# Routed slots of a mixture of experts as pairs and single tiles, the singles in plain float32

## The reference, cut to what matters

```
gate = xt @ Wr + br                      # 1600 tokens, 7 experts
_, ids = top_k(gate + gate_bias, 2)
probs = softmax over the two selected logits
u  = einsum('nh,ehi->eni', xt, Wup) + bup
g  = silu(einsum('eni,eij->enj', u, Wgate) + bgate) * u
eo = einsum('enj,ejh->enh', g, Wdown) + bdown
out = einsum('ne,enh->nh', probs, eo)
out += shared expert of the same form (Wsu, Wsg, Wsd)
x = x + tanh(g_ffn[1]) * out
```

## Time and profile before

| | |
|---|---|
| median of 3 runs | 2024.52 us (2023.42 to 2028.41) |
| profiled execution | 2027.26 us, span 2025.5 us |
| TensorE busy | 1837.5 us, 91% |
| VectorE, ScalarE, GpSimd busy | 1398.9, 974.6, 680.3 us |
| HBM read, written | 156.99 MB, 33.36 MB |

### The profile page before, as it was taken

The page is one execution under the profiler, slowest core; times in us unless marked ns, Lnnn a source line. Parts: engine busy times, 40 slices in busy tenths (PEclk is TensorE's granted clock), DMA queues, the critical chain, the costliest instruction groups (busy, mean ns, idle before and its releaser), DMA issues. The chain is left out here.

```text
span 2025.5 us, 31266 instructions
## 1 busy us (share of the span) xinstructions
PE 1837.5 (91%) x11244; PEld 1445.7 (71%) x11258; DVE 1398.9 (69%) x2821; ACT 974.6 (48%) x2042; POOL 680.3 (34%) x628
## 2 busy tenths in 40 slices
PE   4899999999999899998987997999968899999996
PEld 4677887777877687777763544666538789999996
DVE  5776677777678677888767884677836437666664
ACT  3444444543544344443444654655433236666663
POOL 4332122332623212332101131232322564566553
PEclk9999999999999999999997998999979999999999
DMA  5022201220311321222125111000041457777783
GB/s 203 17 85 82 79 28 62 85 89 1 118 39 36 128 81 37 73 93 97 37 60 212 47 38 42 1 2 1 1 162 38 138 98 231 227 246 239 231 243 74
DMA packets 52397, 192.38 MB, mean 95 GB/s; under 512 B 7678, under 2 KB 11902, under 8 KB 41494
## 3 DMA queue, kind: packets, MB, share of 16 engines
q1 hardware_dynamic: 40550, 167.01, 23.5%
q0 software_dynamic: 11408, 23.37, 6.3%
q10 hardware_dynamic: 288, 0.00, 0.0%
HBM read 156.99 MB, written 33.36 MB: 94 GB/s over the span
## 5 line engine op out<-in xcount | busy, mean ns | idle before, releaser
L363 POOL TENSOR_TENSOR la_q_roped<-la_q_roped 128x400 f32<-128x400 f32 x128 | 139.5, 1111 | 682.5 <-DVE la_q_roped L819 682.5
L722 ACT ACTIVATE la_probs<-banks,la_minus_max 100x361 f32<-100x361 f32 x256 | 144.7, 565 | 195.1 <-DVE la_minus_max L909 195.1
L819 DVE TENSOR_TENSOR la_q_roped<-banks,la_rope_q 128x400 f32<-128x400 f32 x384 | 197.0, 565 | 26.7 <-PE banks L490 16.2
L2072 DVE TENSOR_TENSOR ex_weights_low<-ex_raw_weights,ex_weights_high 128x2048 fp32r<-128x2048 f32 x60 | 137.6, 2293 | 53.4 <-ACT ex_weights_high L1967 50.4
L527 PEld LDWEIGHTS banks<-identity,la_probs 100*121 100x121 f32 x768 | 113.0, 184 | 71.1 <-DVE la_probs L916 45.7
L916 DVE TENSOR_SCALAR la_probs<-la_probs,la_rsum 100x361 f32<-100x361 f32 x256 | 152.2, 595 | 9.1
L538 PE MATMUL banks<-la_probs_t,la_kv_rows 121*128 121x200 f32 x768 | 151.4, 333 | 0.0
L2339 POOL TENSOR_TENSOR ex_g_low<-ex_g,ex_g_high 128x256 fp32r<-128x256 f32 (+1 forms) x104 | 86.7, 950 | 179.1 <-ACT ex_g_high L2011 178.6
L909 DVE TENSOR_REDUCE la_minus_max<-banks 100x1 f32<-100x361 f32 x256 | 134.9, 527 | 16.1 <-PE banks L518 9.4
L527 PE MATMUL banks<-identity,la_probs 100*121 100x100 f32 x768 | 126.1, 273 | 21.8 <-DVE la_probs L916 18.2
L1967 ACT CAST ex_weights_high<-ex_raw_weights 128x2048 fp32r<-128x2048 f32 x60 | 114.2, 1903 | 41.8 <-PE banks L2420 35.1
(11 more groups left out here) (335 smaller groups left out, 5279.3 us busy)
## 6 DMA issues: line engine op xcount, KB each, us to landing
ex_raw_weights<-w_exp SPq DMA_DIRECT2D x60, 1024.0 KB
la_weights<-w_pack SPq DMA_DIRECT2D x15, 1856.0 KB, 7.9
la_kv_turned<-w_ffn SPq DMA_DIRECT2D x30, 384.0 KB
la_rope_k<-w_ffn SPq DMA_DIRECT2D x30, 384.0 KB
qf_sign_weights<-ffn_signs SPq DMA_DIRECT2D x3, 2048.0 KB, 10.2
ffn_signs<-la_ffn_signs SPq DMA_DIRECT2D x30, 192.0 KB, 2.1
residual<-x SPq DMA_DIRECT2D x2, 2048.0 KB, 14.4
out<-ex_block_out POOLq DMA_DIRECT2D x13, 256.0 KB, 5.0
```

The costliest lines, as they stand in the source:

```text
L363: pool.tensor_tensor(roped[:, h, 0, c, :], roped[:, h, 0, c, :], roped[:, h, 1, 1 - c, :], ALU.add).then_inc(b_add, 1)
L722: act.activation(prob[:, s % 4, 0:L], ps[0:S, s % 2, 0:L], ACT.Exp, bias=nmax[:, s % 4:s % 4 + 1], accum_out=sums[:, s % 4:s % 4 + 1]).the ...
L819: dve.tensor_tensor(roped[:, h, v, c, :].rearrange("p (b s) -> p b s", b=GB), ps[:, B_BANKS[k % 2], 0:NT].rearrange("p (b s) -> p b s", b=GB),
L2072: dve.tensor_tensor(wl[:, m, :], raw[:, m, :], wh[:, m, :].bitcast(F32), ALU.subtract).then_inc(w_low[m], 1)
```

## The change

The routed slots are 12 pairs (256 rows, as before) and 7 single tiles of 128, so 31 tiles where there were 38; still 19 blocks, in the order pair, single, pair, single, ..., then five pairs. An expert with an odd number of tiles has its last one in a single. Singles, and the shared block 6, use float32 operands and the unsplit weights: one matmul in place of three passes, no low parts. Their weights have a buffer of their own (`raw_s`) in the space of the residual, once that is stored, and each of their loads waits for the single before (its up, gate or down), in the same SyncE queue. `place` and `own` have more steps. SyncE's stores of normed rows come ahead of the first weight loads, which are issued after tiles 2, 6 and 10, and TensorE does not wait for all small loads at the start. In latent attention x is loaded as 4 + 4 + 8 tiles with norms in three parts, and the sign chunks stand at other places in VectorE's order.

```diff
-                sp.dma_start(core.x_all[:, 0:HB, :], x_in[:, 0:HB, :]).then_inc(x_loaded[0], 16)
+                sp.dma_start(core.x_all[:, 0:GB, :], x_in[:, 0:GB, :]).then_inc(x_loaded[0], 16)
                 sp.dma_start(wts[0][:, 0:W_R], w_pack[0, :, 0:W_R]).then_inc(w_first, 16)
+                sp.dma_start(core.x_all[:, GB:HB, :], x_in[:, GB:HB, :]).then_inc(x_loaded[1], 16)
                 sp.dma_start(trigk_all[:], rope_k).then_inc(tab_k, 16)
                 sp.dma_start(kv_all[:], ctx_in[0]).then_inc(kv_loaded, 16)
                 sp.dma_start(trig[:], rope_q).then_inc(tab_q, 16)
                 sp.dma_start(wts[0][:, W_R:W_ALL], w_pack[0, :, W_R:W_ALL]).then_inc(w_in[0], 16)
-                sp.dma_start(core.x_all[:, HB:B, :], x_in[:, HB:B, :]).then_inc(x_loaded[1], 16)
+                sp.dma_start(core.x_all[:, HB:B, :], x_in[:, HB:B, :]).then_inc(x_loaded[2], 16)
...
                 act.wait_ge(const_ready, 2)
+                std(0)
                 act.wait_ge(w_first, 16)
-                for w, high_part, _low in parts0:
+                for k, (w, high_part, _low) in enumerate(parts0):
                     act.copy(high_part, w).then_inc(w_high, 1)
-                std(0)
-                act.wait_ge(x_rstd, 6)
-                norm(0)
-                norm(1)
-                for t in range(GB):
-                    x_split(t)
-                    norm(t + 2)
+                    if k == 0:
+                        act.wait_ge(x_rstd, 6)
+                        norm(0)
+                        norm(1)
+                        for t in range(GB):
+                            x_split(t)
+                            if t + 2 < GB:
+                                norm(t + 2)
+                        std(1)
+                act.wait_ge(x_rstd, 12)
+                norm(GB)
+                norm(GB + 1)
...
                     rope(n, 0, 2)
+                    chunk(n, 0)
                     low(n, 2)
-                    chunk(n, 0)
                     rope(n, 1, 0)
                     rope(n, 1, 1)
+                    rope(n, 1, 2)
                     chunk(n, 1)
-                    rope(n, 1, 2)
...
                     rope(n, 2, 1)
-                    chunk(n, 2)
                     if n == 0:
-                        variances(1)
+                        variances(2)
                     if starts_half(n):
                         kv_split(n, 4)
                         kv_split(n, 5)
                     rope(n, 2, 2)
+                    chunk(n, 2)
...
-RB = E + (2 * N_TOK - E) // BN
-RT = 2 * RB
+RT = E + (2 * N_TOK - E) // BT
+NP = (RT - E) // 2
+NS = RT - 2 * NP
+RB = NP + NS
...
+def routed_order():
+
+    order = []
+    for k in range(max(NP, NS)):
+        order += [("pair", k)] * (k < NP) + [("single", k)] * (k < NS)
+    return order
+
...
+        old_x = core.x_all[:].rearrange("p b d -> p (b d)")
+        raw_s = old_x[:, 0:MATS * KC * D].rearrange("p (m w) -> p m w", m=MATS)
+        xs, us, gs = (old_x[:, at:at + KC * BT].rearrange("p (k n) -> p k n", k=KC)
+                      for at in range(MATS * KC * D, MATS * KC * D + 3 * KC * BT, KC * BT))
...
-                for m in range(MATS):
-                    load(E, m)
+                    sp.dma_start(bd[32 * k:32 * k + EA, :], b_down).then_inc(bd_in, 16)
+                for t in range(B):
+                    sp.wait_ge(normed[t % 2], t // 2 + 1)
+                    sp.dma_start(rows[t * S:(t + 1) * S, :], xn[:, t % XR, :]).then_inc(rows_out[t % XR], 16)
+                    if t in LOAD_AT:
+                        load(E, LOAD_AT.index(t))
+                    if t == 5:
+                        rows_of(0)
+                    if t == 8:
+                        rows_of(1)
...
+                sp.wait_ge(out_init, 64)
+                for m in range(MATS):
+                    sp.dma_start(raw_s[:, m, :], w_exp[E, m]).then_inc(s_in[m], 16)
                 sp.wait_ge(owners, 2)
-                for v in range(1, RB + 1):
-                    e = sp.value_load(owner_i[0:1, v - 1:v], min_val=0, max_val=E - 1)
+                for j in range(SH, BLOCKS):
+                    k = place_of(j)
+                    e = sp.value_load(owner_i[0:1, k:k + 1], min_val=0, max_val=E - 1)
                     for m in range(MATS):
-                        sp.wait_ge(w_low[m], v)
-                        sp.dma_start(raw[:, m, :], w_exp[bass.ds(e, 1), m].rearrange("e p d -> p (e d)")).then_inc(w_in[m], 16)
-                    if v == 1:
+                        if is_pair(j):
+                            sp.wait_ge(w_low[m], version_of(j))
+                            dst, arrived = raw[:, m, :], w_in[m]
+                        else:
+                            i = single_before(j)
+                            if m == UP:
+                                sp.wait_ge(u_psum, (i + 1) * KC)
+                            elif m == GATE:
+                                sp.wait_ge(g_psum, (i + 1) * KC)
+                            else:
+                                sp.wait_ge(d_psum, first_tile(i + 1))
+                            dst, arrived = raw_s[:, m, :], s_in[m]
+                        sp.dma_start(dst, w_exp[bass.ds(e, 1), m].rearrange("e p d -> p (e d)")).then_inc(arrived, 16)
...
                 def block_high(j):
                     act.wait_ge(t_psum, j + 1)
-                    act.copy(xbh[:, j % 2, :, 0:width(j)], turnb(width(j))).then_inc(xb_high, 1)
+                    if not is_pair(j) and singles_before(j) == 0:
+                        act.wait_ge(out_init, 64)
+                    dst = xbh[:, pairs_before(j) % 2, :, :] if is_pair(j) else xs
+                    act.copy(dst, turnb(width(j))).then_inc(xb_high, 1)
...
+                    step(dve.tensor_scalar(tiles[:], upto[:, :, B - 1], BT / 2 - 0.75, 1.0 / BT, ALU.add, ALU.mult))
+                    step(dve.tensor_scalar(tiles[:], tiles[:], ROUND, None, ALU.add))
+                    step(dve.tensor_scalar(tiles[:], tiles[:], ROUND, None, ALU.subtract))
+                    step(dve.tensor_scalar(pairs[:], tiles[:], 0.5, -0.25, ALU.mult, ALU.add))
+                    step(dve.tensor_scalar(pairs[:], pairs[:], ROUND, None, ALU.add))
+                    step(dve.tensor_scalar(pairs[:], pairs[:], ROUND, None, ALU.subtract))
+                    step(dve.scalar_tensor_tensor(out=odd[:], in0=pairs[:], scalar=-2.0, in1=tiles[:],
+                                                  op0=ALU.mult, op1=ALU.add))
+                    for end, n in ((pair_end, pairs), (odd_end, odd)):
+                        step(dve.tensor_tensor_scan(end[:], restart[:, 0, 1:1 + E], n[:], 0.0, ALU.mult, ALU.add))
+                    step(dve.tensor_tensor(pair_at[:], pair_end[:], pairs[:], ALU.subtract))
+                    step(dve.tensor_scalar(pair_at[:], pair_at[:], float(BN), None, ALU.mult))
+                    step(dve.tensor_tensor(odd_at[:], odd_end[:], odd[:], ALU.subtract))
+                    step(dve.tensor_scalar(odd_at[:], odd_at[:], float(BT), float(NP * BN), ALU.mult, ALU.add))
+                    step(dve.scalar_tensor_tensor(out=odd_at[:], in0=pairs[:], scalar=-float(BN), in1=odd_at[:],
+                                                  op0=ALU.mult, op1=ALU.add))
+                    step(dve.tensor_scalar(pair_rows[:], pairs[:], float(BN), -0.5, ALU.mult, ALU.add))
+                    step(dve.tensor_scalar(shift[:], odd_end[:, E - 1:E], float(BT), None, ALU.mult))
...
+                    step(dve.tensor_tensor(hit[:], earlier[:], each(pair_rows), ALU.is_le))
+                    step(dve.tensor_tensor(biased[:], earlier[:], each(pair_at), ALU.add))
+                    step(dve.tensor_scalar(logit[:], biased[:], NP * BN - 0.5, None, ALU.is_ge))
+                    step(dve.scalar_tensor_tensor(out=biased[:], in0=logit[:], scalar=shift[0:S, 0:1], in1=biased[:],
+                                                  op0=ALU.mult, op1=ALU.add))
+                    step(dve.tensor_tensor(earlier[:], earlier[:], each(odd_at), ALU.add))
+                    step(dve.tensor_tensor(biased[:], biased[:], earlier[:], ALU.subtract))
+                    step(dve.tensor_tensor(biased[:], biased[:], hit[:], ALU.mult))
+                    step(dve.tensor_tensor(earlier[:], earlier[:], biased[:], ALU.add))
...
+                    at, last = seq[:, E + NP:E + RB], odd_end[:, E - 1:E]
+                    step(dve.tensor_copy(index[:, 0:NP], seq[:, E:E + NP]))
+                    step(dve.tensor_scalar(index[:, NP:RB], at, last, None, ALU.subtract))
+                    step(dve.tensor_scalar(index[:, NP:RB], index[:, NP:RB], 0.5, -0.25, ALU.mult, ALU.add))
+                    step(dve.tensor_scalar(index[:, NP:RB], index[:, NP:RB], ROUND, None, ALU.add))
+                    step(dve.tensor_scalar(index[:, NP:RB], index[:, NP:RB], ROUND - NP, None, ALU.subtract))
```

(61 more changed lines are left out.)

209 lines of the change are left out of this document (121 added, 88 removed).

## The result

The changed kernel takes 1978.55 us (median of 4 runs, 1973.56 to 1981.05) where the kernel before takes 2024.83 (4 runs). The ratio is 0.9767, 95% interval 0.9749 to 0.9785: 43.5 to 50.8 us faster. The forecast was 1960, the range 1944 to 1986. The sign and the main mechanism hold, the time is inside the range, and the gain of 46 us is about 0.7 of the 65 that the sum promised.

What follows compares the result with a forecast made beforehand. The prediction took TensorE alone to bound the routed blocks, but not the stage's start. Terms -47 - 6 - 12 - 9 + 8.5 = -65.5 took the profiled 2027.3 us to 1961.8; forecast 1960 against the timed median, range 1944 to 1986.

Steps and rivals of the forecast that it cites:

- Part 1: Routed blocks: seven pairs become singles of 11.5 us against 17.85; 47 us saved with the half block.
- The shared half block: Last stage: this block becomes a float32 single, 13.8 us before and 11.5 after, 2.3 saved.
- The handover: After each single, the next block's gate waits for ScalarE's eviction of down: 0.6 us, range 0 to 2.
- The loads: Routed blocks: weight and row transfers fit, 25.5 of 29.4 us per pair plus single; costed at nothing.
- rival B: Late bursts: the pair's up weights land 3 us late in seven periods, 21 lost, 1981; chance 0.15.
- Part 2: Places and owners: added VectorE steps on the path before the second output, plus slower clock; 8.5 us lost (6 to 12).
- Part 3: Last stage's start: router stores ahead of weight loads gain 9 of the 10.1 us wait for stores.
- Part 4: First stage: moved sign chunks close half the first gap and all the second in seven runs; 12 us gained.
- Part 5: First loads: smaller first load brings first projection about 7 us earlier, first widening 6; gain 6 (0 to 7.5).
- Rival A: Singles' float32 counted in passes costs 4/3 of float32r, so blocks lose 12.5 us: 2018; chance 0.07.
- Rival C: Parts 4 and 5, first stage, give nothing: 18 us lost, 1978; chance 0.12.
- Rival D: TensorE's clock falls to 1.2 GHz in the interleaved pair-single stretch: 103 us cost, 2063; chance 0.04.

Runs made afterwards that it cites:

- cols64: Changed kernel with the singles' up and gate products streaming only 64 of their 128 columns; pair plus single 29.77 us, as with 128 columns.
- bank5: Changed kernel with a single's down product in the second bank of the pair, so only the next gate's second chunk waits for the eviction; 1976.52 us.
- split_files: Changed kernel with GpSimd's subtractions ahead of adds and table entries in blocks 1 to 4, and places cut in two halves, owners in block 2; 1972.39 us.
- stores_back: Changed kernel with router stores again behind weight loads and zeros, and TensorE again waiting for small loads and down biases; 1980.72 us.
- loads_late: Changed kernel with the three shared weight loads after tiles 13, 14 and 15, their casts and subtractions behind the router; 1978.39 us, one execution.
- chunk0_back: Changed kernel with only the first sign chunk of a run back behind the low half; 1977.62 us, one execution.
- run 9: Not an experiment: one of the first stage's 16 runs of rope products, counted from 0; gaps 1.03 and 1.26 us before, first 1.11 after, second gone.
- run 10: Not an experiment: one of the first stage's 16 runs of rope products, counted from 0; TensorE's gap 4.93 us before, 0.78 in the changed kernel.
- run 14: Not an experiment: one of the first stage's 16 runs of rope products, counted from 0; a gap of 2.42 us in the changed kernel.

## Why the prediction was right, and where it was not

- Part 1, the blocks: right, 44.2 of 47. The single's price was 11.5 and is 11.9. The missing 0.4, seven times, is up's hesitation (0.26, which the sum had at nothing), 0.07 in the steps of each of up and gate, and rounding. To read the price of a record as streaming was wrong (`cols64`), and it did no harm only because the 0.109 came from a neighbouring row with a weight load of its own. For float32r passes of 128 columns the prediction itself says that something else sets the step; it did not carry this over.
- The shared half block: part of the 44.2. From its turn to the turn of block 8 it is 29.2 us, before 31.8, so 2.6 where 2.3 was the term.
- The handover: right in size and cause (`bank5`).
- The loads: right. There was no wait for weights in the interleaved stretch, and the queues had room (below: DMA share 0.77, as before), so rival B falls.
- Part 2, the places: right. 8.0 and 8.6 us longer from first turn to turn 3, priced at 8.5, and the cause (28 more steps in VectorE's queue ahead of the second output) goes with `split_files`. The clock's share was taken from the slow transposes of the earlier trace rows, and the slow gate chunks came as said.
- Part 3, the stores: the step that failed most, 9 against 2.6 (3.6 to 6.3 by `stores_back`). It took the 10.12 us as the price of what stood ahead in the queue, and let 9 of it go. The sentence that answers it stands beside it in the prediction: "the same bytes still move". `loads_late` shows the exchange.
- Part 4, the chunks: 12 against 8.5. "The first chunk moves into the 0.56 us that VectorE idles": a chunk is 0.55 + 1.29 us, the low half starts 1.2 late, and the rope product with it. That half term, 3.5, gave 0 (`chunk0_back`; the seven first gaps are 0.6 longer in all). The other term, 7 x 1.26 = 8.8, took run 9 for all seven. The gaps other than the first added up to 13.6 us, 4.93 of it in run 10; after the change they are 3.2, with 3.4 of waiting for GpSimd, so they gave 7.0. The 1.8 us that run 10's rope products no longer lose at the lower clock bring the sum to 8.2. So the term came out near its number by luck: about two thirds of the gain is one late store in one run (4.15 + 1.8 us), which no term had.
- Part 5, the start: 6 against 4.6, inside its bounds.
- The end: 2.2 us that no term had. In all profiles of kernels with singles the way from the last product to the end of the span is 15.7 to 16.2 us, before 13.7 and 13.9. The last rows added to the output start 4.1 us after the last product before and 4.8 after; GpSimd's step from the landing of the add before it to its issue is 0.50 in the kernel before and 0.98 after. Behind the last add GpSimd drains, 4.43 us in both profiles of the kernel before and 5.86 in all twelve of kernels with singles, which is 1.4 of the 2.2 (min, median and max in ns, before and after):

```profile
L1897 POOLq DRAIN  x1: 4434/4434/4434, 2020.9 to 2020.9; - x1
L1980 POOLq DRAIN  x1: 5863/5863/5863, 1965.4 to 1965.4; - x1
```

  What makes the drain longer was not tested.
- Rival A, float32 by passes, falls as a whole and holds for one piece. The Trainium skill ("FP8 and Floating Point Precision", "TensorE Precision Notes") counts four passes for true float32; over three reduced ones that is an estimate of 4/3. In the rows, down at 512 columns cost 3.43 / 2.75 = 1.25, near to it; gate at 128 columns cost 3.57 / 5.31 = 0.67.
- Rival C gave 1978 and the time is 1978.5, yet it is not what happened: parts 4 and 5 gave 13 us, not nothing. Its number was met by what parts 1, 3, 4 and 5 and the end fell short, some 16 us, and by a gain that is 5 us smaller by medians than by the profiles. A time alone would have confirmed the wrong story.
- Rival D falls: the window of the interleaved and the last blocks reads a granted clock of 1.00. Around the table entries it read 0.88 (1604 to 1632 us), as before the change (0.88, 1616 to 1645). The new loss of the last stage is behind the 8.9 us wait. The argument against D, that gaps of 2.4 us leave the clock, doesn't hold in general: behind a gap of 2.42 us in run 14 (to 935.20) the changed kernel's clock reads 0.57 over 4 us, and behind the same gap of 2.42 in its second profile it reads 1.00. D falls by the windows, whose gaps are 0.39 us.

```profile
1632.00:1942.00 310.00, 307.26 (x2149) 275.76 (x2148) 153.53 (x187) 172.74 (x283) 128.54 (x116) 1.00 0.77 240
935.00:939.00 4.00, 3.80 (x9) 1.84 (x9) 3.55 (x7) 0.00 (x0) 2.02 (x2) 0.57 0.02 4
```

## What to carry to other kernels

Before halving a tile, find out whether its step is set by the columns streamed or by the number of records: where records set it, plain float32 with two of them beats three reduced passes (here at 128 columns), where columns do, the passes win (here at 512). One run of a loop is not all runs: add up the gaps of all of them before pricing a term. A wait behind a transfer is gone only when its bytes are gone or moved to where nobody waits; ask who waits for what is now queued behind. Work of one engine that is slipped into an idle slot must fit the slot, or whatever follows it carries the difference.

## What the runs showed of the hardware

- A float32 record of 64 columns with a weight load takes 0.110 us, of 128 columns 0.111, of 512 columns 0.429; a float32r pass takes 0.111 at 128 columns and 0.120 at 256.
- After 8.9 us of idle TensorE the granted clock read 0.50 (1.2 GHz) for 3.3 us, and 12 products took 2.56 us in place of 1.43. After 4.93 us of idleness in the first stage it read 0.51 over 7 us, and 16 products took 4.69 in place of 2.91. After 2.4 us it had stayed at 2.4 GHz once, and after 2.42 us in the same place of the changed kernel it fell in one profile and not in the other.
- The third stage, the same in all kernels, took 223.8 to 224.2 us in some profiles and 226.1 to 226.6 in the others, and nothing between; the first eight runs of the first stage spread over 505.5 to 509.5.
- GpSimd's closing drain took 4.43 us in both profiles of the kernel before and 5.86 in all twelve of kernels with singles.
